# Two GATv2 sweeps of a graph kernel: one comparison for two one-hot tiles, and edge scores by one product and one sum in the row buffer

## The reference

```python
def gatv2_conv(x, src, dst, Wl, Wr, att, b, heads, c_out):
    xl = (x @ Wl).reshape(n, heads, c_out)
    xr = (x @ Wr).reshape(n, heads, c_out)
    e = jax.nn.leaky_relu(xl[src] + xr[dst], 0.2)
    logit = jnp.einsum('ehc,hc->eh', e, att)
    m = jax.ops.segment_max(logit, dst)
    a = jnp.exp(logit - m[dst])
    alpha = a / jax.ops.segment_sum(a, dst)[dst]
    out = jax.ops.segment_sum(alpha[:, :, None] * xl[src], dst)
    return out.reshape(n, heads * c_out) + b
```

## Time and profile before

| | |
|---|---|
| median of 3 runs | 7554.61 us (7548.36 to 7562.02) |
| the profiled execution | 7535.38 us, of which the trace spans 7533.4 |
| busy in it: PE, DVE, POOL, ACT | 5665.6, 5193.9, 3587.6, 3052.1 us |
| first GATv2 sweep, 909 to 1590 us | PE 497.4, DVE 545.3, ACT 419.6, POOL 446.2 us busy of 681 |
| second GATv2 sweep, 1658 to 2505 us | PE 737.4, DVE 703.4, ACT 513.2, POOL 444.8 us busy of 847 |
| mean granted PE clock, whole span | 0.89 of full |

### The profile page before, as it was taken

The page is one execution under the profiler, slowest core; times in us unless marked ns, Lnnn a source line. Parts: engine busy times, 40 slices in busy tenths (PEclk is TensorE's granted clock), DMA queues, the critical chain, the costliest instruction groups (busy, mean ns, idle before and its releaser), DMA issues. The chain is left out here.

```text
span 7533.4 us, 127045 instructions
## 1 busy us (share of the span) xinstructions
PE 5665.6 (75%) x27620; PEld 4473.2 (59%) x27621; DVE 5193.9 (69%) x17560; ACT 3052.1 (41%) x10171; POOL 3587.6 (48%) x3779
## 2 busy tenths in 40 slices
PE   2788377768888578848888897887988886667776
PEld 1566266647777356636666785665866665544455
DVE  7665388858888656657999658998669996543313
ACT  0111166636666356625555235554345552100025
POOL 0667276635555167724666006664036661057730
PEclk9999999989999678869999999999999998866678
DMA  1000211132222134436666216665146663023330
GB/s 30 3 3 3 45 51 46 47 51 74 73 72 74 29 92 106 106 57 214 177 175 172 67 68 186 176 178 132 64 123 175 176 175 81 9 70 105 105 61 17
DMA packets 336625, 690.60 MB, mean 92 GB/s; under 512 B 96716, under 2 KB 193926, under 8 KB 336006
## 3 DMA queue, kind: packets, MB, share of 16 engines
q0 software_dynamic: 209536, 581.61, 29.7%
q1 hardware_dynamic: 120320, 103.02, 4.4%
q10 hardware_dynamic: 6406, 2.28, 0.1%
HBM read 605.77 MB, written 80.89 MB: 91 GB/s over the span
## 5 line engine op out<-in xcount | busy, mean ns | idle before, releaser
L1012 PE MATMUL bank<-arena,onehots 128*128 128x264 f32 (+3 forms) x6496 | 1955.9, 432 | 226.2 <-DVE onehots L851 99.6
L973 PE MATMUL bank<-arena,spreads 128*128 x5568 | 1459.4, 370 | 598.0 <-ACT spreads L1026 255.5
L937 POOL DMA_INDIRECT arena<-tab_l,slot_typed x1392 | 1325.9, 953 | 904.7 <-issue 285.6
L1012 PEld LDWEIGHTS bank<-arena,onehots 128*128 128x128 f32 x6496 | 1296.2, 219 | 552.7 <-issue 166.1
L973 PEld LDWEIGHTS bank<-arena,spreads 128*128 128x128 f32 x5568 | 964.7, 205 | 825.9 <-issue 752.4
L937 POOL DMA_INDIRECT arena<-tab_l,slot_src x928 | 886.7, 956 | 482.7 <-issue 255.3
L1205 DVE TENSOR_TENSOR acc<-acc,bank 128x264 f32 (+3 forms) x1624 | 657.1, 405 | 468.6 <-PE bank L1012 459.1
L1026 ACT ACTIVATE spreads<-bank 128x256 f32<-128x256 f32 x1392 | 524.4, 377 | 905.9 <-PE bank L961 903.6
L1100 DVE TENSOR_TENSOR arena<-arena,bank 128x512 f32<-128x512 f32 x928 | 631.1, 681 | 232.1 <-ACT stats L1048 137.0
L937 POOL DMA_INDIRECT arena<-tab_l0b,slot_src x464 | 444.8, 959 | 479.7 <-ACT arena L1066 253.0
L860 ACT ACTIVATE onehots<-iota_row,slot_loc 128x128 f32<-128x128 f32 x1856 | 632.6, 391 | 17.5 <-PEq L1861 8.3
(11 more groups left out here) (360 smaller groups left out, 9535.9 us busy)
## 6 DMA issues: line engine op xcount, KB each, us to landing
tab_l<-arena SPq DMA_DIRECT2D x150, 384.0 KB, 3.1
arena<-tab_l,slot_typed POOLq DMA_INDIRECT x1392
arena<-tab_l,slot_src POOLq DMA_INDIRECT x928
arena<-tab_l0a,slot_src POOLq DMA_INDIRECT x464
arena<-tab_l0b,slot_src POOLq DMA_INDIRECT x464
rec_dram<-arena POOLq DMA_INDIRECT x417, 2.1
arena<-L_gnn_w SPq DMA_DIRECT2D x6, 1024.0 KB, 10.0
tab_l<-arena SPq DMA_DIRECT2D x25, 132.0 KB, 1.7
```

The costliest lines, as they stand in the source:

```text
L937: pool.indirect_dma_start(out=rows_sb[:, a, t, 0:width], out_offset=None, in_=table[:, :], in_offset=bass.IndirectOffsetOnAxis(ap=index[:, ...
L973: mm = pe.matmul(z[x.k % 2][:, t, 0:cw], spreads[:, x.k % 2, t * P:t * P + P], qtab[:, block_no[w], 0:cw], start=True, stop=not gatv2)
L1012: mm = pe.matmul(sums[x.k % 2], onehots[:, x.a, GT * x.k + t, :], rhs, start=t == 0, stop=t == GT - 1)
```

## The change

It does three things, in `edge_pass` alone:

1. `one_hots` makes both tiles of a pair by one `tensor_tensor` comparison of 256 numbers, with the row of indices repeated over the tiles and each edge's place repeated over the 128 columns, in place of two `tensor_scalar` comparisons of 128. GATv2 and GIN use it.
2. For GATv2 the maximum goes to the free half of `rows_sb` and no longer to the bank. There one product with `att` over the whole pair follows in place of the four instructions, and, after the accumulation on line 1205, one `tensor_reduce` sums each half row into `raw`.
3. PE's target product of GATv2 waits for `leaked` of the pair two before, and no longer for `raw_made`.

```diff
-                for t in (GT * x.k, GT * x.k + 1):
-                    op = dve.tensor_scalar(onehots[:, x.a, t, :], iota_row[:, :], loc[:, ds(BT * x.batch + t, 1)],
-                                           None, ALU.is_equal)
-                op.then_inc(S["oh_made"].sem, 1)
+                t = GT * x.k
+                dve.tensor_tensor(onehots[:, x.a, t:t + GT, :], iota_row[:, :].unsqueeze(1).to_broadcast([P, GT, P]),
+                                  loc[:, ds(BT * x.batch + t, GT)].unsqueeze(2).to_broadcast([P, GT, P]),
+                                  ALU.is_equal).then_inc(S["oh_made"].sem, 1)
...
+                            z_free = S["leaked"] if gatv2 else S["raw_made"]
                             if needed(x.g - 1):
-                                pe.wait_ge(S["raw_made"].sem, S["raw_made"].at(x.g - 1))
+                                pe.wait_ge(z_free.sem, z_free.at(x.g - 1))
...
-                            dve.tensor_tensor(pr, pr, src[:, :, D:D + cw], ALU.max).then_inc(S["leaked"].sem, 1)
+                            dve.tensor_tensor(src[:, :, D:D + cw], pr, src[:, :, D:D + cw], ALU.max)\
+                               .then_inc(S["leaked"].sem, 1)
...
                             dve.wait_ge(S["leaked"].sem, S["leaked"].at(xl.g + 1))
-                            for t in range(GT):
-                                for h in range(2):
-                                    ch = slice(cw // 2 * h, cw // 2 * h + cw // 2)
-                                    op = dve.tensor_tensor_reduce(
-                                        out=z[xl.k % 2][:, t, ch], in0=z[xl.k % 2][:, t, ch], in1=att[:, ch],
-                                        scale=1.0, scalar=0.0, op0=ALU.mult, op1=ALU.add,
-                                        accum_out=r[:, t, h:h + 1])
-                            op.then_inc(S["raw_made"].sem, 1)
+                            dve.tensor_tensor(src[:, :, D:D + cw], src[:, :, D:D + cw],
+                                              att[:, 0:cw].unsqueeze(1).to_broadcast([P, GT, cw]), ALU.mult)\
+                               .then_inc(S["multiplied_rows"].sem, 1)
...
+                        if xl.there and gatv2:
+                            dve.wait_ge(S["multiplied_rows"].sem, S["multiplied_rows"].at(xl.g + 1))
+                            dve.tensor_reduce(r, lane_split(src[:, :, D:D + cw], cw // 2), AX, ALU.add)\
+                               .then_inc(S["raw_made"].sem, 1)
```

More of the change, by code:

```diff
@@ L1266, in edge_pass @@
                 per_group += ("activated", "leaked")
-            if hgt:
+            if hgt or gatv2:
                 per_group += ("multiplied_rows",)
```

## The result

The changed kernel takes 7491.31 us in the median of 8 runs (7430.63 to 7506.59), the kernel before 7552.71 us (8 runs, 7541.97 to 7562.02): ratio 0.9903, 95% interval 0.9874 to 0.9931. That is 61 us faster, where 113 were forecast; the time lies in the range given.

What follows compares the result with a forecast made beforehand. No engine was full: a ring of waits through PE, ACT, DVE and PE bound the GATv2 sweeps. Wide -56 and narrow -57 us made -113, so 7442 us as a median, range 7395 to 7515.

Steps and rivals of the forecast that it cites:

- Part 1: One-hot comparisons on DVE in both GATv2 sweeps: one instruction for two tiles saves 0.07 us a pair; gin sweep zero.
- Part 2: Scores on DVE: product plus sum for four instructions, +0.24 us a pair wide, -0.04 narrow; maximum into SBUF costs zero.
- Part 3: PE's target product waits for the maximum, not the scores: nearly all its wait goes, 3.1 us a batch wide.
- Part 4: DVE's stand before the one-hots at the loop's turn goes with the shorter body: 0.95 us a batch wide.
- Wide: Second GATv2 sweep, rows of 256: new batch 27.0 us, saving 2.0; -56 us, or -28 if the turn's stand stays.
- Narrow: First GATv2 sweep, rows of 128: POOL becomes the bound, 20.5 us a batch, saving 2.1; -57 us.
- over 28 batches: Both GATv2 sweeps: the saving a batch was multiplied by 28, being 29 batches less the ends.
- A: Score work fills DVE, the turn's stand stays: wide -28, narrow -28 to -45 us, 7490 in all; chance 0.20.
- B: DVE instructions with two SBUF inputs held up by POOL's gathers: slower, 7681 at 0.6 us a pair; chance 0.09.
- D: New waits only replace old in the GATv2 sweeps: wide +0.4, narrow -0.4 us a batch, within 15 us; chance 0.06.
- C: Both GATv2 sweeps at their bound, narrow 20.1 and wide 26.1 us a batch: -70 and -81, 7404; chance 0.13.
- Together -113 us: Whole kernel: both GATv2 sweeps' savings taken from the profiled 7535.38 us give 7422 in a profile, 7442 as median.

Runs made afterwards that it cites:

- with hints: Changed kernel with jump-back hints on all engines' GATv2, GAT and HGT loops: 7497.02 us; same hints with early release and four score instructions in row buffer: 7476.16 us.
- the hint alone: Kernel before, with only VectorE's loop of the GATv2 sweeps hinted that its end jumps back to its start: 7530.68 us, ratio 0.9950.
- The pause: Changed kernel with sixteen more small DVE instructions between the wide GATv2 sweep and GAT: 8815.99 us, ratio 0.9838, on the second chip.
- the late release: Changed kernel, but PE again waits for the scores (raw_made) before reusing a bank: 8924.84 us, ratio 0.9956, on the second chip.

## Why the prediction was right in the sweeps and too large in the whole

**Part 1, one-hots.** Right on DVE: the comparison and its follower start 0.33 us apart (2005.42 to 2005.75), as worked out. What it missed is that fewer instructions also meant fewer packets of them (276 to 219): alone the edit gave more than twice what it gave within the change.

**Part 2, scores.** The durations came as taken: 0.70 (product), 0.68 (reduction) and 0.68 (maximum into the row buffer) at 512 numbers; product to accumulation 0.61 us, reduction to the next one-hots 0.60; the reduction's wait lies free under the accumulation, with 0.0 idle. The sign was right in the wide sweep: there VectorE's work for a pair grew by the 0.17 us forecast, and with hints the new form loses 36 us against four instructions, both in the row buffer. The small gain forecast for the narrow sweep (-0.11 us a pair) buys nothing: POOL sets that sweep, and both forms take 605 to 607 us in it with hints.

**Part 3, release.** Right and the main part. PE's 75.0 us went to 9.3, and the new waits are the two foretold: 1.3 us before line 988 (1.6 forecast) and 0.8 before line 954 (0.35 forecast).

**Part 4, the turn.** Right that it goes with the shorter body; its cause is now shown. It was sized too small: I took 23.0 us of stand at face value, -27 in the wide sweep and none apart in the narrow one; by itself it is worth 34 and 36 us in them. Within the whole change it is not a sum on top, as the release takes up some of the same time.

**Sums.** Wide: 27.0 us a batch forecast, 26.7 measured; -56 forecast, -58.2 measured. Narrow: 20.5 forecast, 20.6 to 20.7 measured; but -57 forecast and -44.3 measured. (2.1 x 28 is 59, not 57: a slip of 2 us.) The step that was off is "over 28 batches": my stretch of before, 22.6 us a batch, was slower than the sweep's mean of 648.7 / 29 = 22.4, and the start and end of the sweep gained little; 604.4 / 29 = 20.8, a mean saving of 1.5 a batch, not 2.1. And the 0.4 us that I had called unevenness above POOL's 20.1 is not that: it is POOL's own gather, 0.98 us in the mean instead of 0.95.

**Rivals.** A, that the turn's stand stays, gave 7490, which is the time that came, by luck alone: the stand went. B, that instructions with two SBUF inputs are held by the gathers, did not happen to DVE: the product spans 680 to 750 ns, and the same two-instruction form in the bank was no faster. The reverse did, a little: the gathers of the wide sweep span up to 1442 ns, where before it was 1058. D fell with the 102.5 us. C was not reached: 26.7 in the wide sweep against its 26.1, 20.6 to 20.7 in the narrow one against 20.1.

**The step that failed** is "Together -113 us. The profiled execution took 7535.38 us ... So 7422". It takes for granted that what lies behind the two sweeps stays as long as it was. Of the 56 us between 7422 and 7478, 36 are the GAT sweep, 7 HGT, 13 the narrow sweep's term, and the rest nearly cancels (the HGT part was not followed up). Had GAT run as in the trace of before, the execution would have taken 7442. The two fastest runs of the changed kernel, 7430.63 and 7441.67 us with clocks of 0.898 and 0.893, fit that; its six others have 0.880 to 0.885 and 7478 to 7507. That the 7491 us still lie in the range is owed to its width, which was worked out for rivals within the two sweeps, and to nothing foreseen of GAT.

**Open.** Why the unchanged GAT sweep mostly falls into the lower-clock way once the sweeps ahead of it are faster. The changed kernel, the hint alone, and both kernels with hints all show it, the two profiles of before only for one or two slices of 50 us. It is not the change's code, for one hint in other loops brings it about. The stretch ahead of GAT is the same to 2 us in length and at the same clock (0.50), so by these rows nothing handed over differs that I can name. The pause that was to test it ran where the two ways don't show.

## What to carry to other kernels

Ask first what an engine waits for in the slot, not which is busiest: the release of one buffer ahead of the scores was worth more than any instruction saved (111 of 147 us). When an engine stands for "issue" at the same place of every pass of a loop and the instruction queue's packets go up with the body's length, shorten the body or hint its end before changing the instructions; a form that cost more in itself won here only by being short. And when a forecast ends with "the rest stays", look whether the rest has two ways to run: a sweep whose tensor engine had a mean clock between the two levels gave back 36 of the 102.5 us that other sweeps gained here, and 55 of 70.6 with the hint.

## What the runs showed of the hardware

- A 128-number product-and-sum with accumulator is cheaper with both sources and the output in the row buffer than with one source and the output in PSUM: 0.29 against 0.33 us, its read 0.08 against 0.14. From the timeline of the kernel with hints, start to start:

```profile
2005.58 0.28 DVE L1181 CUSTOM_DVE_ANT_0 arena<-arena,att 128x128 f32<-128x128 f32 x1
2005.79 0.08 DVE L1181 DVE_READ_ACCUMULATOR2_ANT raw<- 128x1 f32 x1
2005.79 0.28 DVE L1181 CUSTOM_DVE_ANT_0 arena<-arena,att 128x128 f32<-128x128 f32 x1
```

  That is 0.21 us, against 0.96 / 4 = 0.24 in the bank.
- The two-instruction form in the row buffer, whose product has two SBUF inputs, lengthens some of POOL's gathers: over the wide sweep their median stays at 955 to 956 ns, the longest goes from 1058 to 1442 ns, the mean over the sweep from 959 to 1016:

```profile
L937 POOL DMA_INDIRECT arena<-tab_l0b,slot_src x432: 947/956/1442, 1661.1 to 2377.7; - x144
```

  On the second chip, with the late release, the same form gives a mean of 998 ns in the row buffer and 968 in the bank; the one-hots alone, which have two SBUF inputs as well, give 964. At the same time the small comparison that was held (0.46 us in the median) is no longer; its median is 0.23:

```profile
L1148 DVE TENSOR_SCALAR spread_cols<-lane_mask,arena x58: 224/228/457, 935.1 to 2390.6; 128x16 f32<-128x16 f32 x58
```

- By the Trainium skill (SBUF — State Buffer, "Who interferes with whom") the guess that tensor-tensor instructions don't hold up descriptor generation is marked as inferred. These rows speak against it in part: most gathers are untouched, some take longer.
- The Trainium skill (Vector Engine (DVE) Microarchitecture Reference, "Points that are easy to get wrong") says that an S2S2D2_STT, a form with two sources, halves its throughput when both lie in SBUF and are not bf16. No row tells whether the instruction that the trace calls CUSTOM_DVE_ANT_0 is of that form; if it is, the trace disagrees: 0.21 us there, 0.24 with a source in PSUM.
- One sweep of unchanged code takes 724 to 792 us on the first and third chip, and PE's mean granted clock in it goes from 0.80 to 0.68 with that.
